# Router, shared perceptron and experts of a decoder as one straight-line stage

## The chip, the cores and the metric

One core of a Trainium2 chip runs the whole program. The metric is the device time of one execution in microseconds (us), lower is better. A core has TensorE (PE in the rows, its weight loads PEld), VectorE (DVE), ScalarE (ACT), GpSimd (POOL) and SyncE (SP, which here only issues DMAs). Each engine runs its own instructions in order; semaphores order them against each other.

## The reference, cut to what matters

The program is a two-layer decoder (16 sequences of 112 tokens, width 256). The change is in the feed-forward part of the first layer, a mixture of 8 experts with two of them per token, and one shared perceptron for all tokens:

```
flat = layernorm(x).reshape(T, D)                 # T = 1792, D = 256
probs = softmax(flat @ router_w.T)                # 8 experts
topk_p, topk_i = top_k(probs, 2)
topk_w = topk_p / maximum(topk_p.sum(-1, keepdims=True), 1e-09)
out = sum over e of _mlp(flat, w_fc[e], w_proj[e]) * combine[:, e:e + 1]
out = out + _mlp(flat, shared_fc, shared_proj)    # _mlp = square(relu(x @ up.T)) @ down.T, inner width 1024
x = x + out
```

## The kernel before, in words

The tokens stand transposed in SBUF (features on partitions): `xT` is the running sum, `hT` the normed input. Tokens go in four groups of 448 (`G`). A `Norm` object splits a group's norm into steps on several engines: `sum_halves`, `average` (a product on PE), `centre`, `square`, `sum_squares`, `variance` (PE), `invert_root`, `scale`. The first three groups are normed in the attention stage before; the last one (`tail`, group `GROUPS - 1`) is left to the router.

Three stages follow each other, each a block of its own. A block ends when all engines have reached its end (line 148 in the rows).

`router`: the last group's norm, then the logits (two products of 112 tokens by 8 experts for each of 16 sequences), then a transpose of every token row into `hrow` (PE, copied by ACT), beside a chain of 36 small operations on DVE (`link`) that picks two experts per token and numbers the slots, with five short visits to PE (lines 2044 to 2055). Its results are `routes.slot` (where each token row goes) and `routes.expert` (which expert each of 35 blocks of 128 slots uses). The block's SP also loads the raw weights of a later stage (`load_last`).

`perceptron` (named `s1`): a hardware loop (`Fori`) over three token groups. Per group, 8 up tiles (two products each, ring of four PSUM banks), ACT's relu, DVE's square, then 8 down tiles. Up tile m needs the relu of tile m - 4. Beside it POOL runs `scatter_tokens`: 32 indirect DMAs that write the token rows to the DRAM array `slots_x`, expert by expert. The fourth group's shared perceptron stands in the stage `join_and_prepare`, behind the experts.

`experts`: straight-line code over 35 blocks. SP loads rows and weights of the first three blocks (`AHEAD_BLOCKS`) when the block has begun, then one more for each result stored. PE transposes the block's rows (`turn`), 16 up products, 8 down products. DVE first measures and POOL rounds the raw weights.

In a row, a product of float32 counts as two records, so an up tile is four. The stage `join_and_prepare` later collects the results with 32 more indirect DMAs on POOL (line 1982); in it DVE's line 1272 adds what PE transposed at line 1153.

## Time and profile before

| what | value |
|---|---|
| median of 3 runs | 1936.63 us (1931.78 to 1939.18) |
| the profiled execution's own time | 1934.31 us |
| its span in the trace | 1932.5 us |
| PE busy | 1714.4 us, 89% |
| DVE / ACT / POOL busy | 887.2 / 863.5 / 325.8 us |
| mean DMA rate | 78 GB/s |

Times in the trace count from the start of the span. The three stages lie between 957 and 1350 us. A row gives the start, the duration, the engine, the line and the operation; behind it, in brackets, how long the engine sat idle before and what ended that.

### The profile page before, as it was taken

To read this page: it belongs to the slowest core of one execution; us is meant where nothing else is said; L and a number is where in the kernel's file an instruction comes from. 1 tells how busy PE (TensorE), PEld (TensorE's weight loads), DVE (VectorE), ACT (ScalarE), POOL (GpSimd) and SP (SyncE) were. 2 spreads that over 40 slices of the span, in tenths; PEclk is the share of its full clock that TensorE was granted. 3 is DMA by queue.
4 is the path that set the end of the run, shared out by engine and by line. 5 is a ranking of instruction groups with operands and counts; after the bars stand their busy time and mean duration, and the time that the engine had idled before them with its cause. 6 is when DMAs were issued, how large, how long until landed. Compare 5 with 4: busy or idle time off the path is not lost. (4 is left out here: it accounts for less than half of the span.)

```text
span 1932.5 us, 33205 instructions
## 1 busy us (share of the span) xinstructions
PE 1714.4 (89%) x13034; PEld 1118.6 (58%) x13034; DVE 887.2 (46%) x1436; ACT 863.5 (45%) x1774; POOL 325.8 (17%) x294
## 2 busy tenths in 40 slices
PE   8999999799899999999788799999487988699965
PEld 3455555554455665656553599998244666466642
DVE  4556556212545555555331211211174677276637
ACT  4243434433455555555321122222244888365656
POOL 0011212112000000000133310000601544111112
PEclk9999999999899999999878899999899899799978
DMA  6000000101100000000111499996359532000001
GB/s 235 1 1 1 1 1 1 50 0 56 29 9 17 17 10 17 18 9 2 35 48 45 170 324 329 329 322 241 94 137 223 114 75 62 20 11 11 2 1 38
DMA packets 147911, 150.03 MB, mean 78 GB/s; under 512 B 69760, under 2 KB 134976, under 8 KB 147760
## 3 DMA queue, kind: packets, MB, share of 16 engines
q1 hardware_dynamic: 144688, 140.59, 23.7%
q0 software_dynamic: 3072, 7.34, 1.3%
q8 instruction: 104, 1.70, 0.4%
q14 instruction: 47, 0.39, 0.1%
HBM read 120.39 MB, written 27.53 MB: 77 GB/s over the span
## 5 line engine op out<-in xcount | busy, mean ns | idle before, releaser
L1002 DVE TENSOR_REDUCE x_negmax<-psum 112x2 f32<-112x878 f32 x128 | 131.2, 1067 | 97.9 <-PE psum L830 97.9
L843 PEld LDWEIGHTS psum<-ident,x_probs 112*125 112x125 f32 (+1 forms) x1024 | 118.2, 169 | 76.3 <-issue 47.8
L843 PE MATMUL psum<-ident,x_probs 112*125 112x112 f32 (+1 forms) x1024 | 140.7, 276 | 15.9 <-DVE x_turned L1008 15.6
L941 ACT ACTIVATE x_probs<-psum,x_negmax 112x439 f32<-112x439 f32 x256 | 146.6, 629 | 16.8 <-DVE x_negmax L1002 16.8
L2268 DVE TENSOR_TENSOR masked<-masked 128x512 f32<-128x512 f32 x70 | 49.1, 701 | 208.9 <-ACT masked L2251 208.9
L2221 PE MATMUL psum<-experts_xb,experts_up 128*128 128x128 f32 x1120 | 132.8, 278 | 7.5 <-DMA experts_down<-in_moe_down 7.5
L2221 PEld LDWEIGHTS psum<-experts_xb,experts_up 128*128 128x128 f32 x1120 | 132.4, 194 | 9.6 <-DMA experts_down<-in_moe_down 7.9
L947 ACT COPY x_turned<-psum 125x448 f32<-125x448 f32 x128 | 68.0, 531 | 146.9 <-PE psum L843 146.0
L2229 PE MATMUL psum<-experts_down,masked 128*128 128x256 f32 x560 | 126.7, 379 | 0.0
L1462 PE MATMUL psum<-fold_full,hT 128*112 128x512 f32 x256 | 113.8, 597 | 1.3 <-DVE fold_part L1762 1.3
L2229 PEld LDWEIGHTS psum<-experts_down,masked 128*128 128x128 f32 x560 | 103.5, 190 | 12.8
L1008 DVE COPY x_turned<-psum 125x448 f32<-125x448 f32 (+1 forms) x128 | 78.8, 616 | 46.5 <-PE psum L843 44.7
L2251 ACT ACTIVATE masked<-psum 128x512 f32<-128x512 f32 x70 | 41.8, 597 | 100.8 <-PE psum L2221 100.8
L854 PE MATMUL psum<-x_turned,x_v 125*32 125x112 f32 (+1 forms) x2048 | 83.0, 267 | 1.5 <-DVE x_turned L1008 1.5
L1462 PEld LDWEIGHTS psum<-fold_full,hT 128*112 128x112 f32 x256 | 44.1, 177 | 61.4 <-issue 59.3
L1650 ACT ACTIVATE second_result<-second_result,a_rowmax 112x112 f32<-112x112 f32 x256 | 74.9, 378 | 7.5 <-DVE a_rowmax L1753 7.5
L1053 POOL TENSOR_TENSOR x_mixT<-x_mixT,x_rden 128x448 f32<-128x448 f32 x16 | 18.1, 1129 | 347.3 <-ACT x_rden L954 347.3
L1644 ACT COPY a_turned<-psum 112x448 f32<-112x448 f32 x64 | 32.4, 532 | 81.9 <-PE psum L1490 81.9
L830 PE MATMUL psum<-x_kT,x_qz 32*112 32x439 f32 x512 | 63.0, 553 | 0.0
L285 DVE TENSOR_TENSOR hT<-hT,sq 128x896 f32<-128x896 f32 x24 | 27.9, 1162 | 76.0 <-ACT sq L279 76.0
L854 PEld LDWEIGHTS psum<-x_turned,x_v 125*32 125x32 f32 (+1 forms) x2048 | 42.6, 107 | 33.7 <-issue 24.7
L1450 PE MATMUL psum<-hT,weights 128*128 128x448 f32 x128 | 55.3, 562 | 6.9 <-issue 4.0
(319 smaller groups left out, 3320.4 us busy)
## 6 DMA issues: line engine op xcount, KB each, us to landing
experts_up<-in_moe_up SPq DMA_DIRECT2D x35, 1024.0 KB, 6.0
experts_down<-in_moe_down SPq DMA_DIRECT2D x35, 1024.0 KB, 8.2
offset_rows<-join_rows SPq DMA_DIRECT2D x16, 784.0 KB, 5.3
hrow<-offset_rows SPq DMA_DIRECT2D x16, 784.0 KB, 5.3
x_ctx<-in_ctxT SPq DMA_DIRECT2D x16, 375.0 KB, 3.2
slots_x<-masked SPq DMA_DIRECT2D x1, 4480.0 KB, 21.3
experts_rows<-slots_x SPq DMA_DIRECT2D x35, 128.0 KB, 2.9
slots_y<-experts_result SPq DMA_DIRECT2D x35, 128.0 KB, 3.3
```

Source lines behind the costliest of these rows:

```text
L830: mm = nc.tensor.matmul(psum[0:T, r, 0:KEYS], qz[rows, n // BATCHES_OF % 2, e, m, t:t + T], kT[rows, n % 2, m], start=False, stop=True, sk ...
L843: mm = nc.tensor.transpose(psum[0:CHUNK_ROWS[c], 4 + i % 2, k * T:(k + 1) * T], probs[:, n % 2, slot_of_head(HG * g + k), c * CHUNK:c * CH ...
L854: mm = nc.tensor.matmul(psum[32 * k:32 * k + 32, 7, g * T:(g + 1) * T], v[0:rows, n % 2, c, HG * g + k, :], turned[0:rows, i % 4, k, :], s ...
L941: nc.scalar.activation(probs[:, n % 2, slot], psum[0:T, slot % 4, 0:KEYS], ACT.Exp, bias=negmax[:, n % 2, slot:slot + 1]).then_inc(exped.s ...
L947: nc.scalar.copy(turned[0:rows, i % 4], psum[0:rows, 4 + i % 2, 0:G].rearrange("p (k t) -> p k t", k=HG)).then_inc(copied_even.sem, 1)
L1002: nc.vector.tensor_reduce(negmax[:, n % 2, 2 * pair:2 * pair + 2], psum[0:T, b:b + 2, 0:KEYS], X, ALU.max, negate=True).then_inc(maxed.sem, 1)
L1008: nc.vector.tensor_copy(turned[0:rows, i % 4], psum[0:rows, 4 + i % 2, 0:G].rearrange("p (k t) -> p k t", k=HG)).then_inc(copied_odd.sem, 1)
L1450: mm = nc.tensor.matmul(psum[:, bank, 0:G], wt["w" + name][:, c, m * P:(m + 1) * P], src, start=c == 0, stop=c == C - 1)
L1462: mm = nc.tensor.matmul(psum[0:T, bank, :], hT[:, c, n * T:(n + 1) * T], taps, start=c == 0, stop=c == C - 1)
L1650: e = nc.scalar.activation(probs[:, n % 2, h], probs[:, n % 2, h], ACT.Exp, bias=rowmax[:, n % 2, h:h + 1])
L2221: mm = nc.tensor.matmul(psum[:, 2 * u + half, m * BLOCK:(m + 1) * BLOCK], up[:, w, c, (half * H4 + m) * P:(half * H4 + m + 1) * P], xb[:, ...
L2229: mm = nc.tensor.matmul(psum[:, 6 + u, 0:D], hidden[:, u, m, :], down[:, w, m, :], start=m == 0, stop=m == M8 - 1)
```

## The change: one block without a loop

`router`, `perceptron` and `experts` become one function `mixture` and one block. The loop over three groups is written out. PE takes the first up tile and most logits between the steps of the last norm, then the transposes and the five visits of the routing chain between the up tiles of group 0. The last norm's two sums move from POOL to DVE. For group 0 ACT makes both relu and square (`square_tile`). SP loads the experts' first weights as soon as `routes.expert` stands, and their rows when the scatter is over. The router's small tiles lie in the third weight buffer of the experts. The scatter waits until all token rows are copied. Two preloads of an activation table are gone. The rounding of the raw weights (POOL) follows the scatter, their measuring (DVE) follows the squares of group 1.

```diff
--- before.py
+++ after.py
-def perceptron(nc, stage, psum, hT, accT, w, groups, beside, load_next=None):
...
-        def group_steps(eng, step):
-            with eng.Fori(0, len(groups)) as g:
-                step(At(0, [(g, 1)]), bass.ds(g * G + groups[0] * G, G))
...
-def router(nc, psum, const, w_router, hT, routes, tail, load_last):
...
+GROUPS_BESIDE = GROUPS - 1
+RANK_AT_TILE, COUNT_AT_TILE, BLOCK_AT_TILE, OFFSET_AT_TILE, BEGIN_AT_TILE = 3, 4, 5, 6, 7
+def mixture(nc, psum, const, routes, w_router, shared, w_up, w_down, hT, accT, sq, spare, tail, zeroed, quant, raw, load_last):
...
+    hidden = sq[:].rearrange("p g c t -> p (g c t)").rearrange("p (m t) -> p m t", m=M8)
+    e_hidden = spare[:, 0:2 * M8 * BLOCK].rearrange("p (u m t) -> p u m t", u=2, m=M8)
+    e_relu = spare[:, 2 * M8 * BLOCK:3 * M8 * BLOCK].rearrange("p (u m t) -> p u m t", u=2, m=H4)
+    relu = spare[:, 2 * M8 * BLOCK:2 * M8 * BLOCK + 2 * G].rearrange("p (u t) -> p u t", u=2)
...
+        e_up = s.sb("up", [P, AHEAD_BLOCKS, C, DFF])
+        e_down = s.sb("down", [P, AHEAD_BLOCKS, M8, D])
+        e_rows = s.sb("rows", [P, AHEAD_BLOCKS, D])
...
+        room = [e_up[:, AHEAD_BLOCKS - 1].rearrange("p c n -> p (c n)"), e_down[:, AHEAD_BLOCKS - 1].rearrange("p k n -> p (k n)")]
...
+        rw = scratch(0, P, C, E)
+        plan = scratch(0, P, T + 3 * P + 1 + BLOCKS)
...
+        def shared_bank(g):
+            return 4 if g < GROUPS_BESIDE - 1 else 6
...
         @block.sync
         def _(sp):
-            def load(k):
+            loaded.inc(sp.dma_start(rw, w_router.rearrange("(c p) e -> p c e", p=P)), 16)
+            loaded.inc(sp.dma_start(plan, const["plan"]), 16)
+            sp.wait_ge(loaded.sem, 32)
+            load_last(sp)
+
+            def load_weights(k):
                 n, u = At(k), k % AHEAD_BLOCKS
...
-                sp.dma_start(rows[:, u], routes.slots_x[k * BLOCK:(k + 1) * BLOCK, :]).then_inc(rows_loaded.sem(n), 16)
-                sp.dma_start(up[:, u], w_up[bass.ds(e, 1)].rearrange("o (c p) n -> p (o c) n", p=P)).then_inc(loaded.sem(n), 16)
-                sp.dma_start(down[:, u], w_down[bass.ds(e, 1)].rearrange("o (k p) n -> p (o k) n", p=P)).then_inc(loaded.sem(n), 16)
+                sp.dma_start(e_up[:, u], w_up[bass.ds(e, 1)].rearrange("o (c p) n -> p (o c) n", p=P)).then_inc(weights_loaded.sem(n), 16)
+                sp.dma_start(e_down[:, u], w_down[bass.ds(e, 1)].rearrange("o (k p) n -> p (o k) n", p=P)).then_inc(weights_loaded.sem(n), 16)
+
+            def load_rows(k):
+                n, u = At(k), k % AHEAD_BLOCKS
+                sp.dma_start(e_rows[:, u], routes.slots_x[k * BLOCK:(k + 1) * BLOCK, :]).then_inc(rows_loaded.sem(n), 16)
...
-            sp.wait_ge(routes.scattered.sem, routes.scattered.n)
+            sp.wait_ge(chain.sem, LINKS)
             for k in range(AHEAD_BLOCKS):
-                load(k)
+                load_weights(k)
+            sp.wait_ge(routes.scattered.sem, 16 * 2 * NB)
+            for k in range(AHEAD_BLOCKS):
+                load_rows(k)
             for k in range(BLOCKS):
                 store(k)
                 if k + AHEAD_BLOCKS < BLOCKS:
-                    load(k + AHEAD_BLOCKS)
+                    load_rows(k + AHEAD_BLOCKS)
+                    load_weights(k + AHEAD_BLOCKS)
...
         @block.gpsimd
         def _(pool):
-            beside(pool)
+            Scope.clear_retired(pool)
+            pool.wait_ge(zeroed.sem, zeroed.n)
+            pool.wait_ge(rows_read, NB // 2)
+            for k in range(2):
+                pool.wait_ge(chain.sem, FIRST_SLOTS if k == 0 else LINKS - 1)
+                for b in range(NB):
+                    routes.scattered.inc(nc.gpsimd.indirect_dma_start(
+                        routes.slots_x, bass.IndirectOffsetOnAxis(ap=routes.slot[k][:, b:b + 1], axis=0), hrow[:, b, :], None), 16)
+            round_weights(nc, pool, quant, raw)
...
+            def logits(some):
+                for b in some:
+                    for c in range(C):
+                        mm = nc.tensor.matmul(psum[0:T, 6, b * E:(b + 1) * E], hT[:, c, b * T:(b + 1) * T], rw[:, c, :], start=c == 0, stop=c == C - 1)
+                return mm
+
+            def turn_pair(q):
+                if q >= 2:
+                    pe.wait_ge(rows_read, q - 1)
+                for b in (2 * q, 2 * q + 1):
+                    for c in range(C):
+                        mm = nc.tensor.transpose(psum[0:T, 4 + q % 2, (b % 2) * D + c * P:(b % 2) * D + (c + 1) * P], hT[:, c, b * T:(b + 1) * T], const["ident"][:])
+                mm.then_inc(rows_made, 1)
+
+            def up_tile(g, m):
+                if g * M8 + m >= 4:
+                    pe.wait_ge(relu_made, g * M8 + m - 3)
+                for c in range(C):
+                    mm = nc.tensor.matmul(psum[:, m % 4, 0:G], up[:, c, m * P:(m + 1) * P], hT[:, c, g * G:(g + 1) * G], start=c == 0, stop=c == C - 1)
+                mm.then_inc(up_made, 1)
+
+            def down_tile(g, k):
+                pe.wait_ge(hidden_made, g * M8 + k + 1)
+                for m in range(C):
+                    mm = nc.tensor.matmul(psum[:, shared_bank(g) + m, 0:G], down[:, k, m * P:(m + 1) * P], hidden[:, k], start=k == 0, stop=k == M8 - 1)
+                mm.then_inc(down_made, 1)
+
+            def routing(i):
+                if i == RANK_AT_TILE:
+                    flat_picks = picks.rearrange("p e b -> p (e b)")
+                    pe.wait_ge(chain.sem, PICKED)
+                    nc.tensor.matmul(psum[0:T, 7, 0:P], before, flat_picks, start=True, stop=False)
+                    nc.tensor.matmul(psum[:, 6, COUNTS:COUNTS + 1], flat_picks, ones[0:T, :], start=True, stop=True).then_inc(counted, 1)
+                if i == COUNT_AT_TILE:
+                    pe.wait_ge(chain.sem, COUNTED)
+                    nc.tensor.matmul(psum[:, 6, COUNTS + 1:COUNTS + 2], same, count, start=True, stop=True).then_inc(counted, 1)
+                if i == BLOCK_AT_TILE:
+                    pe.wait_ge(chain.sem, BLOCKED)
+                    nc.tensor.matmul(psum[:, 6, COUNTS + 2:COUNTS + 3], lower, col[:, 2:3], start=True, stop=True)
+                    nc.tensor.matmul(psum[:, 6, COUNTS + 3:COUNTS + 4], earlier, count, start=True, stop=True).then_inc(counted, 1)
+                if i == OFFSET_AT_TILE:
+                    pe.wait_ge(chain.sem, OFFSET)
+                    nc.tensor.matmul(psum[0:T, 7, 0:P], offset, const["ident"][:], start=False, stop=True).then_inc(counted, 1)
+                if i == BEGIN_AT_TILE:
+                    pe.wait_ge(chain.sem, BEGUN)
+                    nc.tensor.matmul(psum[0:1, 6, 2 * P:2 * P + BLOCKS], ones, begun, start=True, stop=True).then_inc(counted, 1)
             def turn(k):
 
                 n = At(k)
                 pe.wait_ge(*rows_loaded.after(n))
                 pe.wait_ge(*xb_ready.after(n - 1))
+                if k == 0:
+                    pe.wait_ge(shared_added, GROUPS_BESIDE - 1)
...
-            turn(0)
+            shared.wait(pe)
+            tail.average(pe, LAST, 7)
+            up_tile(0, 0)
+            pe.wait_ge(loaded.sem, 32)
+            pe.wait_ge(*tail.ready(LAST - 1))
+            logits(range(0, 5))
+            tail.variance(pe, LAST, 7)
+            logits(range(5, 12))
+            pe.wait_ge(*tail.ready(LAST))
+            logits(range(12, NB)).then_inc(scored, 1)
+            for m in range(M8):
+                if m:
+                    up_tile(0, m)
+                turn_pair(m)
+                routing(m)
+            pe.wait_ge(rows_read, NB // 2)
+            for k in range(M8):
+                down_tile(0, k)
+            for g in range(1, GROUPS_BESIDE):
+                for m in range(M8):
+                    up_tile(g, m)
+                if g == 1:
+                    pe.wait_ge(shared_added, 1)
+                else:
+                    pe.wait_ge(chain.sem, LINKS)
+                for k in range(M8):
+                    if g == GROUPS_BESIDE - 1 and k == H4:
+                        turn(0)
+                    down_tile(g, k)
+
...
-                pe.wait_ge(*loaded.after(n))
+                pe.wait_ge(*weights_loaded.after(n))
...
+                if k == 0:
+                    pe.wait_ge(shared_added, GROUPS_BESIDE)
...
-            xb_ready.start(act)
-            result_ready.start(act)
-            relu_done.start(act)
-            nc.scalar.preload_act_table(ACT.Relu)
+            for x in (xb_ready, result_ready, relu_done):
+                x.start(act)
+
+            def relu_tile(g, m):
+                i = g * M8 + m
+                act.wait_ge(up_made, i + 1)
+                if i >= 2:
+                    act.wait_ge(hidden_made, i - 1)
+                nc.scalar.activation(relu[:, m % 2], psum[:, m % 4, 0:G], ACT.Relu).then_inc(relu_made, 1)
+
+            def square_tile(m):
+
+                act.wait_ge(relu_made, m + 1)
+                act.wait_ge(*tail.ready(LAST))
+                nc.scalar.activation(hidden[:, m], relu[:, m % 2], ACT.Square).then_inc(hidden_made, 1)
+
+            tail.square(act, LAST)
+            relu_tile(0, 0)
+            tail.invert_root(act, LAST, 7)
+            act.wait_ge(chain.sem, 2)
+            nc.scalar.activation(t["prob"], t["shifted"], ACT.Exp).then_inc(exped, 1)
+            for m in range(M8):
+                if m:
+                    relu_tile(0, m)
+                square_tile(m)
+                act.wait_ge(rows_made, m + 1)
+                nc.scalar.copy(hrow[:, 2 * m:2 * m + 2].rearrange("p b d -> p (b d)"), psum[0:T, 4 + m % 2, 0:2 * D]).then_inc(rows_read, 1)
+            for g in range(1, GROUPS_BESIDE):
+                for m in range(M8):
+                    relu_tile(g, m)
...
             take(0)
+            act.wait_ge(hidden_made, GROUPS_BESIDE * M8)
...
-            dve_first(dve)
             hidden_ready.start(dve)
...
+            tail.sum_halves(dve, LAST, nc.vector)
+            nc.vector.memset(ones, 1.0)
+            tail.centre(dve, LAST, 7)
+            tail.sum_squares(dve, LAST, nc.vector)
+            tail.scale(dve, LAST)
+            dve.wait_ge(scored, 1)
+            logits = psum[0:T, 6, 0:NB * E].rearrange("p (b e) -> p b e", e=E)
...
+            def add_shared(g):
+                dve.wait_ge(down_made, M8 * (g + 1))
+                x = accT[:, :, g * G:(g + 1) * G]
+                b = shared_bank(g)
+                nc.vector.tensor_tensor(x, x, psum[:, b:b + C, 0:G], ALU.add).then_inc(shared_added, 1)
+
+            add_shared(0)
+            for g in range(1, GROUPS_BESIDE):
+                for m in range(M8):
+                    dve.wait_ge(relu_made, g * M8 + m + 1)
+                    dve.wait_ge(down_made, (g - 1) * M8 + m + 1)
+                    nc.vector.tensor_tensor(hidden[:, m], relu[:, m % 2], relu[:, m % 2], ALU.mult).then_inc(hidden_made, 1)
+                if g == 1:
+                    measure_weights(nc, dve, quant, raw)
+                add_shared(g)
             for k in range(BLOCKS):
                 n, u = At(k), k % 2
...
-                router(nc, psum, const, a["router_w"], hT, routes, n4,
-                       lambda sp: load_to_quantise(nc, sp, quant, raw, {x: a["q_" + x] for x in ("gate", "up", "down", "clip_x", "clip_down")}))
-                perceptron(nc, "s1", psum, hT, xT, shared, range(GROUPS - 1), lambda pool: scatter_tokens(nc, pool, routes, zeroed))
-                experts(nc, psum, const, routes, a["moe_up"], a["moe_down"],
-                        lambda dve: measure_weights(nc, dve, quant, raw), lambda pool: round_weights(nc, pool, quant, raw), masked[:].bitcast(F32))
+                mixture(nc, psum, const, routes, a["router_w"], shared, a["moe_up"], a["moe_down"], hT, xT, sq, masked[:].bitcast(F32), n4, zeroed, quant, raw,
+                        lambda sp: load_to_quantise(nc, sp, quant, raw, {x: a["q_" + x] for x in ("gate", "up", "down", "clip_x", "clip_down")}))
```

The order of PE's instructions, as the built programs have it, from the last norm's average to the experts. Before (names: `router_rw` is the router's weight, `s_hidden` the perceptron's inner tile, `L665` its loop):

```order
L256 MATMUL psum<-sq,averager 128x448
L273 MATMUL psum<-sq,averager 128x448
L2033 MATMUL psum<-router_rw,hT 112x8 x32
L2040 MATMUL psum<-ident,hT 112x128 x32
L2044 MATMUL psum<-router_picks,router_plan 112x128
...
L148 UNCONDITIONAL_BRANCH
...
L689 MATMUL psum<-hT,weights 128x448 x2
...
L665 COMPARE_AND_BRANCH
```

After (`mix_up` holds the router's weight and scratch, `hT,weights` is an up tile, `sq,weights` a down tile):

```order
L256 MATMUL psum<-sq,averager 128x448
L2046 MATMUL psum<-hT,weights 128x448 x2
L2031 MATMUL psum<-mix_up,hT 112x8 x10
L273 MATMUL psum<-sq,averager 128x448
L2031 MATMUL psum<-mix_up,hT 112x8 x22
L2039 MATMUL psum<-ident,hT 112x128 x4
L2046 MATMUL psum<-hT,weights 128x448 x2
...
L2052 MATMUL psum<-sq,weights 128x448 x16
L2046 MATMUL psum<-hT,weights 128x448 x16
L2052 MATMUL psum<-sq,weights 128x448 x8
L2083 MATMUL psum<-ident,mix_rows 128x128 x2
```

The first up tile and ten of the 32 logit products now stand ahead of the variance, the transposes are spread over the up tiles, and the experts' first turn stands in the middle of the last down tiles. No branch is left between them.

The order of SP's instructions behind the raw weights, after the change (`mix_down` is the experts' second weight, `mix_rows` the rows of a block):

```order
L2322 DMA raw_weights<-in_q_down 128x2x704
L1982 TENSOR_LOAD block_expert
L1984 ISA
L1984 DMA mix_up<-in_moe_up 128x2x1024
L1985 DMA mix_down<-in_moe_down 128x8x256
...
L1989 DMA mix_rows<-slots_x 128x256 x3
L1995 DMA slots_y<-mix_result 128x256
```

Before, the rows of each block were loaded directly ahead of its weights, behind the block's branch.

## Rows read from the trace of the kernel before

**Rows 1.** Timeline, PE, the three stages: start, duration, engine, line, idle before.

```profile
995.96 14.29 PE L689 MATMUL psum<-hT,weights 128*128 x32 [3.38 <-ACTq L74]
1010.09 12.19 PE L695 MATMUL psum<-s_hidden,weights 128*128 128x448 f32 x32
1022.11 6.18 PE L689 MATMUL psum<-hT,weights 128*128 x16
1029.45 1.77 PE L689 MATMUL psum<-hT,weights 128*128 x4 [1.16 <-issue]
1038.60 7.88 PE L689 MATMUL psum<-hT,weights 128*128 x12 [7.38 <-issue]
...
1058.34 12.19 PE L689 MATMUL psum<-hT,weights 128*128 x32
...
1094.83 5.82 PE L2221 MATMUL psum<-experts_xb,experts_up 128*128 128x128 f32 x32 [7.47 <-DMA experts_down<-in_moe_down]
...
1104.15 3.73 PE L2221 MATMUL psum<-experts_xb,experts_up 128*128 128x128 f32 x32
...
1343.24 3.73 PE L2221 MATMUL psum<-experts_xb,experts_up 128*128 128x128 f32 x32
```

**Rows 2.** Windows: stretch, length, busy time by engine, PEclk, DMA share, GB/s.

```profile
970.00:982.00 12.00, 11.84 (x64) 11.84 (x65) 0.11 (x1) 0.00 (x0) 0.00 (x0) 0.50 0.01 1
...
1000.00:1022.00 22.00, 22.00 (x60) 11.15 (x59) 5.00 (x8) 3.80 (x7) 17.12 (x17) 1.00 0.29 88
...
1101.00:1340.00 239.00, 239.00 (x1651) 225.28 (x1650) 46.29 (x66) 60.31 (x133) 18.81 (x25) 1.00 0.95 322
```

**Rows 3.** Timeline, the last norm, 957 to 970.

```profile
957.35 0.06 DVE L2077 MEMSET router_ones<- 128x1 f32 x1 [0.35 <-PEq L148]
...
960.64 1.83 PE L256 MATMUL psum<-sq,averager 128*128 128x448 f32 x2 [4.49 <-POOL sq L252]
...
965.84 1.86 PE L273 MATMUL psum<-sq,averager 128*128 128x448 f32 x2 [3.37 <-POOL sq L269]
...
969.01 1.09 DVE L285 TENSOR_TENSOR hT<-hT,sq 128x896 f32<-128x896 f32 x1 [5.42 <-ACT sq L279]
```

**Rows 4.** Timeline, logits, transposes and the routing chain.

```profile
970.16 12.11 PE L2033 MATMUL psum<-router_rw,hT 128*112 128x8 f32 x64 [2.46 <-DVE hT L285]
...
982.13 5.74 PE L2040 MATMUL psum<-ident,hT 128*112 128x128 f32 x32
...
987.88 0.38 DVE L2101 TENSOR_TENSOR router_picks<-router_pick 112x128 f32<-112x128 f32 x1
...
994.59 0.18 DVE L2131 TENSOR_SCALAR block_expert<-psum 1x35 uint32<-1x35 f32 x1
```

**Rows 5.** Timeline, POOL's scatter and ACT's relu in the second group.

```profile
996.05 1.15 POOL L1974 DMA_INDIRECT slots_x<-hrow,slot  x1 [30.26 <-SPq L148]
...
1008.19 1.20 POOL L1974 DMA_INDIRECT slots_x<-hrow,slot  x1 [0.30 <-issue]
...
1028.85 0.54 ACT L709 ACTIVATE s_relu<-psum 128x448 f32<-128x448 f32 x1 [18.02 <-PE psum L689]
...
1036.36 0.94 POOL L1974 DMA_INDIRECT slots_x<-hrow,slot  x1 [0.30 <-issue]
...
1038.01 0.54 ACT L709 ACTIVATE s_relu<-psum 128x448 f32<-128x448 f32 x1 [8.61 <-remote]
```

**Rows 6.** Timeline, the stage behind the experts, beside the last indirect DMAs.

```profile
1380.50 0.41 PE L1153 MATMUL psum<-ident,hrow 112*128 112x112 f32 x2 [3.38 <-issue]
...
1398.82 0.39 DVE L1272 TENSOR_TENSOR xT<-xT,psum 128x224 f32<-128x224 f32 x1 [18.38 <-remote]
1399.24 0.62 DVE L252 TENSOR_TENSOR sq<-xT 128x448 f32<-128x448 f32 x1
```

**Rows 7.** DMA queues in the window 1011 to 1084: packets, MB, share.

```profile
DMA packets 1056, 2.52 MB, mean 35 GB/s; under 512 B 352, under 2 KB 352, under 8 KB 1056
## 3 DMA queue, kind: packets, MB, share of 16 engines
q0 software_dynamic: 1056, 2.52, 11.2%
```

More of the change, by code:

```diff
@@ L2137 @@
[L2137 to L2155 removed]
+        ones = scratch(0, P, 1)
```

300 lines of the change are left out of this document (91 added, 209 removed).

## The prediction

> **What bounds the kernel now.** I read the windows first, then the timeline of each engine through the three stages. In the 35 expert blocks PE is busy 239 of 239 us at the full clock [rows 2], and a block takes (1343.24 - 1104.15) / 33 = 7.24 us [rows 1]. Nothing there changes, so the change can win only ahead of them, between the barrier at 957.3 [rows 3] and the first expert product at 1094.83 [rows 1]. PE waits or crawls there in four places. The last norm goes back and forth between engines for 13 us, with PE idle in it [rows 3]. The logits and transposes run for 12.1 and 5.7 us at half clock while nothing else does; the routing chain goes on to 994.59 [rows 2, 4]. The perceptron's second group takes 1058.34 - 1022.11 = 36.2 us, where two rounds of 12.02 us (1022.11 - 1010.09) are its work: 12.2 us are lost [rows 1]. And from about 1082.4 (1058.34 and two rounds) to 1094.83 PE has only one turn to do and waits for the experts' weights; then the first block runs at half clock, 9.32 us to the next block in place of 7.24 [rows 1].
>
> **The loss in the second group** decides most of the answer. PE has finished the first up tile of that group near 1023.8 (22.11 and four records of 0.376). ACT's relu of it starts at 1028.85, and the next at 1038.01, though its tile was done some 12 us before [rows 1, 5]. PE can take only four tiles ahead, so it stops. All of this lies beside the 32 indirect DMAs, 996.05 to 1036.36 [rows 5]. The same sight stands in the stage behind the experts, which has no loop there: PE transposes at 1380.50, and DVE, which waits for that transpose alone, starts at 1398.82, 18.4 us idle [rows 6]. I read both as one thing: while POOL issues indirect DMAs, what waits for PE's results can be released many microseconds late. PE is then held only where it needs an answer, so in the up tiles, not in the down tiles.
>
> Another reading is the loop: its second pass needs code from further back. The third pass, which branches back in the same way, loses nothing (1058.34 is on time) [rows 1]. The DMA queues moved no instruction packet from 1011 to 1084 [rows 7]. So I give the branch little. The Trainium skill, page "Runtime: NRT & Kernel Launch", section "Instruction fetch mechanics", says the opposite: a taken branch whose target is not in the current two-page window makes the engine wait for a DMA fetch, and kernels should be unrolled. By it the whole 12.2 us would go with the loop; the absence of instruction packets in this trace speaks against it here.
>
> **The change part by part.**
>
> 1. The norm. The sum moves to DVE, 0.62 us [rows 6], and can start at the barrier, 957.35 [rows 3]. PE's average then starts at about 958.1 in place of 960.64. PE's own list to the end of the logits is now the limit: average 1.8 [rows 3], one up tile at half clock 3.0 (twice 1.5), 64 logit records 12.1 [rows 4], variance about 1.6. Together 18.5, so they end at 976.6 and not at 982.3. The norm itself fits: variance done near 968.5, scale about 2.4 later (965.84 + 1.86 to 970.10) [rows 3], at 970.9, while the middle logits run to 973.6. The clock stayed at 0.50 all through the logits [rows 2]; should the up tile lift it, 4 us more are won. Gain 5.7.
>
> 2. Group 0's up tiles under the routing. From 976.6 PE has 7 up tiles (10.5), the transposes (5.7), seven small products (0.36 each, like two records of the transposes [rows 4], 2.5) and a cold start (14.29 - 12.19 = 2.1 [rows 1]). That is 20.8; the transposes behind the clock's rise are shorter, so I take 20, to 996.6. The picks stand 988.26 - 982.3 = 6 us after the logits [rows 4], and PE asks for them only after three up tiles: no wait. But each of the chain's later visits to PE now waits behind an up tile and a pair, 2.2 us. So the experts' numbers stand at about 997.5, not earlier than before (994.8), and the scatter starts at about 997, where it was at 996.05 [rows 4, 5]. What is won is that 12 us of up tiles are done by then. ACT has relu, square and copy, under 1.8 us, in each 2.2.
>
> 3. Down tiles of group 0 to 1009, group 1 to 1033.1, group 2 to 1057.2, the turn in it 0.4: PE is free for the experts at 1057.6 if nothing stalls. The first weights (6 DMAs of 1 MB, issued from about 998) have until then, and the rows have from the scatter's end, about 1041, to the turn at 1051. DVE's measuring of the raw weights lies beside group 1's down tiles (12 us), POOL's rounding behind the scatter; neither is asked for by PE. The two table loads (ACT) lay beside waits already: zero.
>
> 4. The barriers and the cold first block. The block follows at once and at full clock: 9.32 - 7.24 = 2.1 us.
>
> Without a stall: 1094.83 - 1057.6 + 2.1 = 39.3 us. The stall stays, because the scatter stays and lies at the same time: 997 to 1038. Before it cost 12.2. It can now fall on group 1's up tiles (1009 to 1021) and the first ones of group 2 (1033). From below: if the late releases begin 26 us into the scatter as before (1022), only group 2 meets them, for 3 to 6 us. From above: in the later stage they held three times in a row until the DMAs ended; if group 1 is caught at its fourth tile (1015) and freed at about 1042.5, what is left is 18.1 + 24.1 + 0.4 and a cold start of 2.1, so the experts begin at 1087. I take 12, the size of the one stall in the same code. Sum: 39.3 - 12 = 27 us. Against the profiled execution's 1934.3 that is 1907; against the median, which lies 2.3 higher, 1909.5.
>
> **The rivals.**
>
> - The stall goes or is small, by the loop's branch or by timing. For it: the unrolled code, and half of before's scatter passed without a late release (to 1022). Against it: the loopless stage [rows 6]. Gain 33 to 39, with a warmer start 43: 1894 to 1904. Chance 0.25.
> - The long stall: group 1 is held until the scatter is over. For it: the 18.4 us of [rows 6], and the weights' 6 MB now move beside the scatter. Then 1094.83 - 1087.1 + 2.1 = 10 us gain, with half of it held 20: 1917 to 1927. Chance 0.23.
> - Slower: the scatter itself is stretched. A DMA issue took 1.20 + 0.30 us beside a busy DVE where it took 0.94 + 0.30 otherwise [rows 5]. With all 32 at 1.5 us it lasts 48 in place of 41 us, and on top of the long stall the experts start at 1094: no change. PE waits in order, so everything behind the turn waits for the rows too. It is slower from the point where the scatter ends later than about 1052 (1.7 us a DMA); if the 6 MB beside it double the issue, to 2.5 us, it ends at 1077, and the time is about 1960. Nothing in the trace shows such a rate. Chance 0.05, and 0.07 for no change.
> - The forecast, a stall between 6 and 17 us: 1902 to 1916. Chance 0.40.
>
> **How the numbers follow.** The likeliest case gives 1909. The range takes the forecast, the small stall and the long one but for their ends: 1894 to 1926. About 0.5%, 9.7 us, is what a measurement of this kernel can tell from no change. Faster by more than that: 0.40 + 0.25 + nearly all of 0.23 = 0.87. Within it: 0.07 and the end of the long stall, 0.08. Slower: 0.05.
>
> **What would show it.** PE's logits end near 976.6 and the seven small products stand between up tiles, with no wait over 1 us. POOL's first indirect DMA starts at 995 to 999, 32 of them at 1.25 us. The weights' issues stand beside it. ACT's relus of group 1 or 2 start several microseconds after their tile, and PE's up tiles show the gap; the down tiles show none. The first expert product starts at 1066 to 1074, at full clock, and the blocks keep 7.24 us. I am wrong if the gap is missing (then the start is at 1058), if the up tiles of group 1 end only when the scatter does (1087), if the scatter's issues are longer than 1.25 us, or if the routing chain falls behind the up tiles so far that the third group waits for it.

## The result, and the profile after

The changed kernel took 1904.23 us (median of 4, 1901.80 to 1906.97) where the kernel before took 1934.72 us beside it (median of 4): a ratio of 0.984, 95% interval 0.982 to 0.986, 30.5 us less. The profiled execution took 1906.97 us with a span of 1905.1 us. The forecast was 1909.0 us, with 1894 to 1926 as its range.

The runs of this work were made on four occasions, not all on one chip, and the kernel before itself took 1934.7, 1891.9, 1933.6 and 1932.7 us on them. Only kernels of one occasion are compared below, except where a sentence says otherwise; they are called the first (the result above) to the fourth occasion.

PE through the changed stage, its timeline, which answers to [rows 1, 3, 4]:

```profile
957.85 0.99 PE L256 MATMUL psum<-sq,averager 128*128 128x448 f32 x2 [2.03 <-DVE sq L252]
958.67 3.06 PE L2046 MATMUL psum<-hT,weights 128*128 128x448 f32 x4
961.53 2.37 PE L2031 MATMUL psum<-mix_up,hT 128*112 128x8 f32 x20
...
964.59 7.30 PE L2031 MATMUL psum<-mix_up,hT 128*112 128x8 f32 x44
971.75 1.08 PE L2039 MATMUL psum<-ident,hT 128*112 128x128 f32 x4
972.62 3.19 PE L2046 MATMUL psum<-hT,weights 128*128 128x448 f32 x4
...
990.61 12.29 PE L2052 MATMUL psum<-sq,weights 128*128 128x448 f32 x32 [1.12 <-ACT hrow L2165]
1002.74 12.43 PE L2046 MATMUL psum<-hT,weights 128*128 128x448 f32 x32
1015.00 6.18 PE L2052 MATMUL psum<-sq,weights 128*128 128x448 f32 x16
...
1037.89 4.66 PE L2052 MATMUL psum<-sq,weights 128*128 128x448 f32 x8 [3.76 <-DVE sq L2273]
1042.39 12.19 PE L2046 MATMUL psum<-hT,weights 128*128 128x448 f32 x32
...
1066.66 3.73 PE L2124 MATMUL psum<-mix_xb,mix_up 128*128 128x128 f32 x32
...
1074.13 3.73 PE L2124 MATMUL psum<-mix_xb,mix_up 128*128 128x128 f32 x32
...
1313.21 3.73 PE L2124 MATMUL psum<-mix_xb,mix_up 128*128 128x128 f32 x32
```

The logits now end at 971.75, group 0's down tiles begin at 990.61, and its whole perceptron is done at 1002.74. Group 1 (up tiles from 1002.74, down tiles from 1015.00) runs to 1042.39, 39.65 us where two rounds are 24.05: the gap of [rows 1] is still there, 15.6 us of it. Then nothing holds PE until the experts, and their first block is nearly a normal one, 7.47 us; the blocks keep (1313.21 - 1074.13) / 33 = 7.24 us.

Windows (us; the columns are busy time and instructions of PE, PEld, DVE, ACT and POOL, then PE's granted clock, DMA share and GB/s), against [rows 2]:

```profile
961.50:963.90 2.40, 2.40 (x22) 2.37 (x21) 0.11 (x1) 0.54 (x1) 0.00 (x0) 0.85 0.94 310
...
968.00:971.70 3.70, 3.70 (x21) 3.70 (x22) 0.00 (x0) 0.00 (x0) 0.00 (x0) 0.50 0.24 93
```

Behind the one up tile the clock is granted at 0.85 under the first logits; under the last ones it is back at 0.50.

ACT and POOL in the timeline, against [rows 5], and DVE in the stage behind the experts, against [rows 6]:

```profile
1012.80 0.54 ACT L2147 ACTIVATE masked<-psum 128x448 f32<-128x448 f32 x1 [3.02 <-PE psum L2046]
1020.52 0.54 ACT L2147 ACTIVATE masked<-psum 128x448 f32<-128x448 f32 x1 [7.18 <-issue]
1029.62 0.54 ACT L2147 ACTIVATE masked<-psum 128x448 f32<-128x448 f32 x1 [8.56 <-remote]
1036.63 0.98 ACT L2147 ACTIVATE masked<-psum 128x448 f32<-128x448 f32 x2 [6.47 <-remote]
...
991.44 1.15 POOL L2019 DMA_INDIRECT slots_x<-hrow,slot  x1 [41.79 <-ACT hrow L2165]
...
1030.74 0.95 POOL L2019 DMA_INDIRECT slots_x<-hrow,slot  x1 [0.30 <-issue]
...
1362.43 0.39 DVE L1192 TENSOR_TENSOR xT<-xT,psum 128x224 f32<-128x224 f32 x1 [14.23 <-remote]
```

PE has all eight up tiles of group 1 done at 1015.0. ACT's relus of the last four start at 1020.52, 1029.62 and (two) 1036.63. PE, by now in the down tiles, waits for what comes of them. The scatter runs from 991.44 to 1031.69, 32 DMAs at 1.25 us.

### The profile page after: what moved, and what is told of

Same layout as the page of the kernel before. It is cut to its first block and busy times, and to the rows that moved or that the text cites. A ratio compares the mean times of both kernels' runs of the same rounds, so it can differ in the third digit from the quotient of the medians.

```text
span 1905.1 us, 33059 instructions
## 1 busy us (share of the span) xinstructions
PE 1710.4 (90%) x13034; PEld 1113.8 (58%) x13034; DVE 883.6 (46%) x1430; ACT 865.5 (45%) x1780; POOL 324.0 (17%) x292
## 3 DMA queue, kind: packets, MB, share of 16 engines
q1 hardware_dynamic: 144688, 140.59, 24.1%
## 5 line engine op out<-in xcount | busy, mean ns | idle before, releaser
L763 PE MATMUL psum<-ident,x_probs 112*125 112x112 f32 (+1 forms) x1024 | 140.8, 276 | 15.9 <-DVE x_turned L928 15.6
L2124 PEld LDWEIGHTS psum<-mix_xb,mix_up 128*128 128x128 f32 x1120 | 130.6, 192 | 2.1 <-issue 0.4
L2124 PE MATMUL psum<-mix_xb,mix_up 128*128 128x128 f32 x1120 | 130.7, 275 | 0.0
L2134 PE MATMUL psum<-mix_down,masked 128*128 128x256 f32 x560 | 126.9, 379 | 0.0
L2134 PEld LDWEIGHTS psum<-mix_down,masked 128*128 128x128 f32 x560 | 103.6, 190 | 13.0 <-DVE masked L2282 0.4
```

Source lines behind the costliest of these rows:

```text
L763: mm = nc.tensor.transpose(psum[0:CHUNK_ROWS[c], 4 + i % 2, k * T:(k + 1) * T], probs[:, n % 2, slot_of_head(HG * g + k), c * CHUNK:c * CH ...
L2124: mm = nc.tensor.matmul(psum[:, 2 * u + half, m * BLOCK:(m + 1) * BLOCK], e_up[:, w, c, (half * H4 + m) * P:(half * H4 + m + 1) * P], xb[: ...
L2134: mm = nc.tensor.matmul(psum[:, 6 + u, 0:D], e_hidden[:, u, m, :], e_down[:, w, m, :], start=m == 0, stop=m == M8 - 1)
```

## The experiments

### The scatter and the late releases, first try

Theory A: what holds PE in group 1 is that its results are released late beside POOL's indirect DMAs. Four kernels were run on the second occasion. The changed kernel without the scatter, so that the experts work on rows of zeros (SP then waits only for that zeroing before it loads rows):

```diff
-            sp.wait_ge(routes.scattered.sem, 16 * 2 * NB)
+            sp.wait_ge(zeroed.sem, zeroed.n)
...
-            for k in range(2):
-                pool.wait_ge(chain.sem, FIRST_SLOTS if k == 0 else LINKS - 1)
-                for b in range(NB):
-                    routes.scattered.inc(nc.gpsimd.indirect_dma_start(...), 16)
+            pool.wait_ge(chain.sem, LINKS - 1)
             round_weights(nc, pool, quant, raw)
```

> The changed kernel without the 32 indirect DMAs that scatter the token rows; the experts compute on the zeroed rows instead, with the same blocks and weights. Theory A (results of PE are released late while POOL issues indirect DMAs): group 1 takes 24.1 us in place of 39.65, the first expert product starts near 1051, and the time falls by about 15.5 us, to 1888.5. Rival B (the hold is from the order of the code, such as the square on DVE behind the sum of group 0, or the experts' weight loads beside): group 1 stays at 35 to 40 us and the time moves by under 4 us.

The 32 DMAs as plain ones to fixed places, on POOL's queue:

```diff
-                    routes.scattered.inc(nc.gpsimd.indirect_dma_start(...), 16)
+                    routes.scattered.inc(nc.gpsimd.dma_start(routes.slots_x[(k * NB + b) * T:(k * NB + b + 1) * T, :], hrow[:, b, :]), 16)
```

> The changed kernel with each indirect DMA replaced by a plain one of the same size (112 rows of 1 KB to a fixed place), issued by POOL at the same point. Theory A1 (it is the software-made descriptors of POOL's queue): group 1 still takes 35 to 42 us. Theory A2 (it is the indirect form alone): group 1 takes 24 to 26 us, and the first expert product starts near 1051.

The same 32 plain DMAs on SP's queue, behind the first weights (POOL's loop over them is gone, as in the first kernel):

```diff
+            sp.wait_ge(rows_read, NB // 2)
...
+                    routes.scattered.inc(sp.dma_start(routes.slots_x[(k * NB + b) * T:(k * NB + b + 1) * T, :], hrow[:, b, :]), 16)
```

> The changed kernel with the 32 scatters replaced by plain DMAs of the same size on SP's queue, behind the first weights. Theory A1: no late release, group 1 at 24 to 26 us, first expert product 1051 to 1056. Rival C (any DMA traffic of this size beside the up tiles holds PE's releases): group 1 still takes over 30 us.

And the kernel before without its scatter:

```diff
-            sp.wait_ge(routes.scattered.sem, routes.scattered.n)
...
-                perceptron(nc, "s1", psum, hT, xT, shared, range(GROUPS - 1), lambda pool: scatter_tokens(nc, pool, routes, zeroed))
+                perceptron(nc, "s1", psum, hT, xT, shared, range(GROUPS - 1), lambda pool: pool.wait_ge(zeroed.sem, zeroed.n))
```

> The kernel before with its loop over three groups, without the 32 indirect DMAs (the experts compute on zeroed rows). Theory A: the second pass of the loop starts its relu on time, the second group takes 24.1 us in place of 36.2, and the time falls by 12 us, to about 1923. Rival D (the branch back of the loop costs it): the second group still takes about 36 us, and the time does not move.

Measured: 1859.87 us (4 runs, ratio to the kernel before 0.984, 0.980 to 0.988), 1858.93 and 1858.36 us (one run each), and 1890.29 us (10 runs, ratio 1.000, 0.998 to 1.001). Group 1 took 24.05 us in the first three, the second group 24.05 us in the last. Taken alone, this seems to say that the scatter costs nothing. But look at the stage behind the experts, whose 32 indirect gathers all four kernels keep. The trace of the changed kernel without the scatter, DVE and then PE in that stage:

```profile
1334.09 0.39 DVE L1192 TENSOR_TENSOR xT<-xT,psum 128x224 f32<-128x224 f32 x1 [0.50 <-PE psum L1073]
...
1309.53 9.26 PE L1059 MATMUL psum<-hT,weights 128*128 128x448 f32 x24 [2.78 <-PEq L148]
...
1338.88 1.37 PE L1087 MATMUL psum<-hT,weights 128*128 128x448 f32 x3 [0.85 <-DVE hT L285]
```

From its first up tile to the first product of line 1087 that stage takes 29.35 us here, and 58.99 us (1323.19 to 1382.18) in the changed kernel on the first occasion; DVE's waits for its first transposes are 0.5 to 2.1 us, where the longest was 14 to 18. Here nothing is released late even beside indirect DMAs, so the kernel before has no gap to lose either (hence 1.000), and the four runs can't tell theory A from its rivals. What they do show: late releases are no property of the program alone. In the kernel before itself the stage behind the experts takes 57.97 us on the first occasion (1353.22 to 1411.19) and 31.15 us here without the scatter (1341.04 to 1372.19). These 26.8 us and the 12.2 us of the second group are 39.0 of the 42.8 us by which the kernel before is faster here.

### The scatter and the late releases, second try

The first and the fourth kernel were run again on the fourth occasion.

> The changed kernel without its 32 scattering DMAs, so the experts work on rows that are zero; all else stands. The same file as the first experiment, sent again so that it meets a chip where the kernel before takes near 1935 us. Theory A: group 1 takes 24.1 us in place of 36 to 40, the first expert product starts near 1051 to 1053, and the time is 12 to 15 us less than the changed kernel's. Rival (the weights' 6 MB or the measuring of the raw weights beside group 1 is what holds it): group 1 stays at over 30 us and the time within 4 us.

> The kernel before, with its loop, without its 32 scattering DMAs, so the experts work on rows that are zero. The same file as the fourth experiment, sent again for the same reason. Theory A: its second group takes 24.1 us in place of 36.2, branch and all, and the time is about 12 us less than the kernel's before, a ratio of 0.994. Rival (the loop's branch back costs the 12 us): the second group still takes 34 to 37 us, ratio 1.000.

The first took 1884.85 us (4 runs, ratio 0.977, 0.973 to 0.981), the second 1919.09 us (5 runs, ratio 0.993, 0.990 to 0.995), 13.6 us less than the kernel before. PE's timeline of the changed kernel without the scatter:

```profile
956.45 0.99 PE L256 MATMUL psum<-sq,averager 128*128 128x448 f32 x2 [2.03 <-DVE sq L252]
...
1001.33 12.19 PE L2042 MATMUL psum<-hT,weights 128*128 128x448 f32 x32
...
1025.39 12.19 PE L2042 MATMUL psum<-hT,weights 128*128 128x448 f32 x32
...
1049.66 3.73 PE L2120 MATMUL psum<-mix_xb,mix_up 128*128 128x128 f32 x32
...
1305.96 10.71 PE L1059 MATMUL psum<-hT,weights 128*128 128x448 f32 x24 [2.78 <-PEq L148]
...
1364.36 1.74 PE L1087 MATMUL psum<-hT,weights 128*128 128x448 f32 x4 [0.85 <-DVE hT L285]
```

and of the kernel before without it:

```profile
1021.21 12.19 PE L689 MATMUL psum<-hT,weights 128*128 x32
...
1045.26 12.19 PE L689 MATMUL psum<-hT,weights 128*128 x32
...
1080.39 5.57 PE L2220 MATMUL psum<-experts_xb,experts_up 128*128 128x128 f32 x32 [6.44 <-DMA experts_down<-in_moe_down]
```

Both groups fall to 24.05 us. The stage behind the experts, which keeps its 32 gathers, takes 58.40 us (1305.96 to 1364.36) and not 29.35: results are released late on this occasion too, and the loss is gone only where the indirect DMAs are. The loop's branch back is still in the second kernel, so it costs nothing that shows, and that rival is out. The weights' 6 MB and the measuring of the raw weights are still in the first one, so by themselves they hold nothing. From the norm's average to the first expert product the changed kernel takes 93.2 us here; with the scatter it takes 108.8 (957.85 to 1066.66, first occasion) or 105.7 (third, below): the scatter costs it 12.5 to 15.6 us, and it cost the kernel before 13.6. Without any scatter the change is worth 1919.09 - 1884.85 = 34.2 us. The saving doesn't depend on the stall. Whether plain DMAs of POOL would release late as well on such a chip wasn't tried.

### The changed kernel with parts undone

On the third occasion, beside the changed kernel itself.

> The changed kernel itself, unchanged, beside the kernel before on the same chip. Where the kernel before takes near 1892 us, and its second group has no gap, theory A (the saving in front of the experts comes from the order of work, and is nearly the same with and without late releases) expects group 1 in 24.1 us, the first expert product near 1052 us, and a time of 1860 us, a ratio of 0.983. The rival, that the scatter costs something in the changed kernel even there, expects 1865 to 1875 us and a gap in group 1 or 2. Where the kernel before takes near 1935 us, both expect group 1 in 36 to 42 us and 1904 us.

1896.46 us (4 runs, 1891.94 to 1902.01), ratio 0.980 (0.978 to 0.983): results are released late here, and the same program takes 1896 us where it took 1904 on the first occasion. Its timeline is the base for the next three:

```profile
956.36 0.99 PE L256 MATMUL psum<-sq,averager 128*128 128x448 f32 x2 [2.04 <-DVE sq L252]
...
989.12 12.29 PE L2052 MATMUL psum<-sq,weights 128*128 128x448 f32 x32 [1.12 <-ACT hrow L2165]
1001.25 12.19 PE L2046 MATMUL psum<-hT,weights 128*128 128x448 f32 x32
...
1037.76 12.19 PE L2046 MATMUL psum<-hT,weights 128*128 128x448 f32 x32
...
1062.03 3.73 PE L2124 MATMUL psum<-mix_xb,mix_up 128*128 128x128 f32 x32
```

**The router's work first, then group 0.** (ACT's order follows.)

```diff
             tail.average(pe, LAST, 7)
-            up_tile(0, 0)
+            tail.variance(pe, LAST, 7)
             pe.wait_ge(loaded.sem, 32)
...
-            logits(range(12, NB)).then_inc(scored, 1)
+            logits(range(NB)).then_inc(scored, 1)
             for m in range(M8):
-                if m:
-                    up_tile(0, m)
                 turn_pair(m)
+            for m in range(M8):
                 routing(m)
+            for m in range(M8):
+                up_tile(0, m)
```

> Undoes one part: in the stage without a loop the logits, all 16 transposes and the routing chain's seven small products come ahead of every up tile of group 0, as they did before; the shared groups are still unrolled, the barriers are still gone and the weights are still loaded beside. Theory: the interleaving is worth what the order says, the up tiles under the chain: the down tiles of group 0 start 12 to 15 us later than in the changed kernel, and so do the first expert product and the end: +12 to +15 us on the changed kernel, most of its saving gone on a chip where nothing is released late. Where releases are late the scatter starts up to 6 us earlier, against work that starts later, and the difference may fall to 8 us. Rival: the saving is that of the missing barriers, the loop and the early weights, and the interleaving gives under 4 us.

1914.81 us (4 runs), ratio 0.991 (0.989 to 0.993), 18.4 us more than the changed kernel.

```profile
956.35 0.99 PE L256 MATMUL psum<-sq,averager 128*128 128x448 f32 x2 [2.03 <-DVE sq L252]
...
1000.92 12.19 PE L2052 MATMUL psum<-sq,weights 128*128 128x448 f32 x32
1012.95 5.80 PE L2046 MATMUL psum<-hT,weights 128*128 128x448 f32 x15
...
1034.59 8.52 PE L2046 MATMUL psum<-hT,weights 128*128 128x448 f32 x16 [14.27 <-ACT masked L2144]
...
1054.96 12.19 PE L2046 MATMUL psum<-hT,weights 128*128 128x448 f32 x32
...
1079.24 3.73 PE L2121 MATMUL psum<-mix_xb,mix_up 128*128 128x128 f32 x32
```

The down tiles of group 0 start 11.8 us later, as the order says. The scatter now catches group 1 in its up tiles: PE stands still behind its fourth tile until 1034.59, and the group takes 42.0 us where it took 36.5. So 17.2 us are lost by the first expert product: 11.8 of order, 5.4 of a worse meeting with the scatter. The expectation that the stall would give some of it back was wrong in sign. The interleaving is about half of the whole saving, 18.4 of 37.2 us on this occasion. The other half (DVE's sums, the barriers and the wait for weights behind them) is read from the timelines; no run takes it apart.

**The first weights behind the scatter.**

```diff
-            for k in range(AHEAD_BLOCKS):
-                load_weights(k)
             sp.wait_ge(routes.scattered.sem, 16 * 2 * NB)
             for k in range(AHEAD_BLOCKS):
                 load_rows(k)
+                load_weights(k)
```

> Undoes one part: the weights of the first three expert blocks are issued behind the scatter, with the blocks' rows, and not beside the picks. Theory: the scatter's last DMA is issued near 1031 us, the six transfers of 1 MB land in 15 to 20 us from there, the first block's two within 8, and the first product is due at 1052 (no late releases) or 1067 (late releases): 0 to +2 us on the changed kernel. Rival: the weights are what the experts would wait for, as in the kernel before, whose PE waited from about 1082 to 1095; then +5 to +12 us.

1903.88 us (4 runs), ratio 0.983 (0.980 to 0.986). The median is 7.4 us above the changed kernel's, more than the 0 to 2 us expected, but the intervals of the two ratios overlap (0.980 to 0.986 and 0.978 to 0.983), and the timeline places no loss in front of the experts:

```profile
957.83 1.00 PE L256 MATMUL psum<-sq,averager 128*128 128x448 f32 x2 [2.03 <-DVE sq L252]
...
1063.62 3.73 PE L2123 MATMUL psum<-mix_xb,mix_up 128*128 128x128 f32 x32
```

That is 105.79 us from the average to the experts, and 105.67 in the changed kernel; to the first up tile of the stage behind the experts it is 362.45 us (957.83 to 1320.28) and 362.34 (956.36 to 1318.70). What the profiled executions differ by lies outside the changed stage. Loading the first weights early is worth nothing here: from the scatter's end (1032.06) to the first expert product PE has 31.6 us of other work and of stall, which hide them anyway. Whether they would be hidden without the stall isn't shown.

**No up tile ahead of the logits.**

```diff
-            up_tile(0, 0)
             pe.wait_ge(loaded.sem, 32)
...
-                if m:
-                    up_tile(0, m)
+                up_tile(0, m)
```

> Group 0's first up tile no longer stands ahead of the logits, but behind them with the others. Theory (that dense tile is what raised the clock under the logits): the 64 logit records go back to 0.189 us each, 12.1 us in all, the granted clock is 0.50 under them as in the kernel before, and the down tiles of group 0 start 1 to 4 us later than in the changed kernel. Rival: the clock rises for another reason, the logits take 9.7 us as in the changed kernel, and the down tiles start at the same time or up to 1 us earlier or later.

1906.39 us (one run). The timeline:

```profile
958.82 0.99 PE L256 MATMUL psum<-sq,averager 128*128 128x448 f32 x2 [2.03 <-DVE sq L252]
961.21 3.90 PE L2031 MATMUL psum<-mix_up,hT 128*112 128x8 f32 x20 [1.40 <-DMA mix_up<-in_plan]
964.97 1.84 PE L273 MATMUL psum<-sq,averager 128*128 128x448 f32 x2
966.60 8.25 PE L2031 MATMUL psum<-mix_up,hT 128*112 128x8 f32 x44
...
995.82 12.29 PE L2052 MATMUL psum<-sq,weights 128*128 128x448 f32 x32 [1.13 <-ACT hrow L2161]
```

The logits take 3.90 + 8.25 = 12.15 us again, all at a granted clock of 0.50, and the down tiles start 37.0 us behind the average in place of 32.8: 4.2 us later. The logits are 2.5 us of it (12.15 against 2.37 + 7.31), the variance 0.8, and PE idles 1.40 us ahead of the logits for a table that the tile used to cover; 0.5 us of these 4.7 comes back behind the logits. One dense tile ahead of the logits is what lifted the clock for them.

### Fewer signals from PE

In the changed kernel's late stretch ACT's relus start further and further behind their tiles. Theory B: PE's increments stand in a queue that drains slowly, so fewer of them would wait less.

```diff
-                mm.then_inc(up_made, 1)
+                if g == 0:
+                    mm.then_inc(up_made, 1)
+                elif m % 2:
+                    mm.then_inc(up_made, 2)
...
-                mm.then_inc(down_made, 1)
+                if k == M8 - 1:
+                    mm.then_inc(down_made, M8)
```

> The changed kernel with fewer signals from PE in the stage without a loop, and no other edit: groups 1 and 2 tell of two up tiles at once (one increment by 2), and a group's eight down tiles are told of once, at the last (an increment by 8). Theory B (beside the indirect DMAs PE's increments are released one behind another, some 3.5 us apart at first and 7 to 9 later, so what counts is how many stand in that queue): group 1 then has 4 such increments for its up tiles in place of 8, the relus start within 1 to 4 us of their tiles, group 1 takes 25 to 30 us in place of 36 to 40, and the time is 6 to 12 us less than the changed kernel's, on a chip where the kernel before takes near 1935 us. Where it takes near 1892 us: no difference. Rival (each release is late by a time of its own until the DMAs end, however many there are): group 1 takes 36 to 40 us as before, within 2 us of the changed kernel.

The second kernel has the same edit also in the stage behind the experts.

> The kernel with fewer signals, and the same edit also in the stage behind the experts (its up tiles told of in pairs, its eight down tiles at the last). Theory B: that stage has the same queue beside its 32 gathers, and loses about 28 us there; 16 of its some 25 increments become 5, so it gives 8 to 15 us more than the kernel with the edit in one stage. Rival: the transposes between the tiles need an answer each, are late by a time of their own, and it gives under 3 us. Near 1892 us for the kernel before: no difference.

On the fourth occasion 1900.75 us (4 runs, ratio 0.985, 0.981 to 0.988) and 1900.88 us (4 runs, ratio 0.985, 0.981 to 0.988). ACT and PE of the first of the two:

```profile
1001.88 0.98 ACT L2151 ACTIVATE masked<-psum 128x448 f32<-128x448 f32 x2 [15.39 <-issue]
1007.05 0.98 ACT L2151 ACTIVATE masked<-psum 128x448 f32<-128x448 f32 x2 [4.20 <-remote]
1016.88 0.98 ACT L2151 ACTIVATE masked<-psum 128x448 f32<-128x448 f32 x2 [8.85 <-remote]
1030.88 0.98 ACT L2151 ACTIVATE masked<-psum 128x448 f32<-128x448 f32 x2 [13.03 <-remote]
...
998.67 12.26 PE L2046 MATMUL psum<-hT,weights 128*128 128x448 f32 x32
...
1037.58 12.19 PE L2046 MATMUL psum<-hT,weights 128*128 128x448 f32 x32
```

The pairs of tiles are done at 1001.8, 1004.8, 1007.8 and 1010.8; the relus follow after 0.1, 2.3, 9.1 and 20.1 us. In the changed kernel (third occasion) the relus of the same tiles, the second, fourth, sixth and eighth, follow after 0.2, 3.0, 10.6 and 21.6 us. So the lag goes with the tile and not with the number of signals sent before it, and group 1 takes 38.9 us, inside the 36.5 to 39.7 of the changed kernel. Theory B falls. The stage behind the experts gains 0.7 us by the same edit (57.9 to 57.2 us from its first up tile to the first product of line 1087, 1089 in the second), not 8 to 15. Neither kernel is shown to be faster than the changed one.

What fits all the traces is simpler: the last late result is released a few us after POOL's last indirect DMA, 4.9 us behind it in the changed kernel (1031.69 to 1036.63), 2.7 here (its last DMA ends at 1028.15), 5.3 with the router first (1028.67 to 1033.99). In the kernel before, the last DMA ends at 1037.30 [rows 5], and the last late relus, of tiles done by 1028.1, start 4.2 us later:

```profile
1041.47 0.98 ACT L709 ACTIVATE s_relu<-psum 128x448 f32<-128x448 f32 x2 [2.92 <-remote]
```

Behind the experts, in all ten traces of the three occasions, DVE's last late start comes 3.7 to 5.7 us after the last gather. So PE is free a few us behind the last DMA, plus what it still has to do then. This is read from the traces and was not tested by itself; why results are held back stays open.

## Why the prediction was right

The time was forecast within 5 us. That is closer than its parts were: the first two terms gave 5.9 us more than forecast and the stall took 3.6 us more, so part of the closeness is luck. Times by which the changed kernel is ahead on the first occasion, from [rows 1, 4] and the timeline above: end of the logits 10.4 (982.13 against 971.75), down tiles of group 0 19.5, up tiles of group 1 19.4, up tiles of group 2 16.0, first expert product 28.2, last expert block 30.0.

1. **The norm and the logits**: forecast 5.7 us, measured 10.5. This is the mis-sized term. The sum did start when the barrier fell (average 957.85, forecast 958.1), and PE's list was the limit. But the logits took 9.7 us and not 12.1, the variance 1.0 and not 1.6, because the up tile lifted the clock. The average took 0.99 us and not 1.8; that isn't the tile's doing, since it took 0.99 without the tile too. PE had idled 2.03 us before it, and 4.49 in the kernel before [rows 3], whose 1.8 us I had carried over. The prediction named 4 us for the clock and did not take them, since the clock had stayed at 0.50 under the logits of before; without the tile 4.2 us are lost, 3.3 of them by the clock under logits and variance.
2. **The up tiles under the routing**: forecast 20 us, measured 18.9 (971.75 to 990.61). The seven small products stand between the tiles with no wait; the one wait is 1.12 us for ACT's last copy, ahead of the down tiles. The scatter came at 991.44, 4.6 us before it did in the kernel before, outside the 995 to 999 that I had named: since the whole list was shorter, the token rows were copied and the slots known earlier.
3. **The three groups**: down tiles, up tiles and the turn are as costed, and nothing that PE asks for waits for the weights, DVE's measuring or POOL's rounding. Where the first weights stand turned out to be free either way.
4. **The barriers and the cold first block**: forecast 2.1 us, measured 1.85 (9.32 against 7.47). The wait for weights ahead of it is gone: 1082.4 to 1094.83 before, nothing now. Without the scatter the kernel before still waits there (6.44 us for the weights, and then 5.57 us for the first block's up products, which take 3.73 in a later block), so that part belongs to the change and not to the stall.
5. **The stall**: forecast 12 us, measured 15.6 on the first occasion and 12.5 on the third (1001.25 to 1037.76). The cause was right, by the second try. The place was not: I wrote that PE is held in the up tiles, not in the down tiles, and that the down tiles show no gap. They show all of it. PE's up tiles of group 1 ran through (12.43 us), since only ACT's first four relus are needed for them: the fourth was 4 us late, at 1012.80, and just early enough for the eighth tile. The down tiles need what comes of the last four. I had overlooked that a down tile waits for an answer too, through relu and square. The gap stands in the up tiles where the scatter is further on when group 1 begins: 24.1 us with the router first (988.86 to 1012.95), for 5.4 us more, and 11.3 us in the changed kernel (989.95 to 1001.25, same occasion).

The sum closes: 27.3 forecast, plus 4.8 and 1.1 for terms 1 and 2, minus 3.6 for the stall, is 29.6; measured are 30.0 at the last expert block, 27.4 in the span of the two profiled executions and 30.5 between the medians.

Of the rivals, the small stall did not come. Its first reason fails, since the loop's branch costs nothing. Its second is half true: here too the first part of the scatter passes almost in time, and the first relu that is 4 us late starts at 1012.80, 21 us into it, but group 1 lay right there. The Trainium skill's rule on taken branches (page "Runtime: NRT & Kernel Launch", section "Instruction fetch mechanics"), weighed in the prediction, has no price here: the pass behind the branch takes 24.05 us, two rounds of work. That doesn't contradict the rule, which speaks of targets outside a window; no run shows whether this loop's start lies inside. The long stall had its mechanism right, held until the DMAs end, but when the last result came PE had only one or two down tiles of group 1 left, and group 2, and not a group and a half. The stretched scatter did not come: 1.25 us a DMA beside the weights' 6 MB.

## What to carry to other kernels

Put work that PE can do in any order between the steps of a chain that other engines set; it was worth 11.8 us here, 17.2 with what the stall added, and dense tiles also keep the clock up for the small products between them. An early load gives nothing where the work behind it is long enough to hide it (31.6 us here). A stall that ends with another queue's last transfer is sized by that end and by the work that is left then, so ask what an earlier start of the waiting work will meet there.

## What the runs showed of the hardware

- **Late releases came on three of the four occasions.** There, beside 32 indirect DMAs of POOL, results of PE are released up to some 20 us late, the last ones 2.7 to 5.7 us after the last DMA. On the second occasion, on another chip than the third and the fourth, the trace shows nothing of the kind (29.35 against 58.99 us for the stage behind the experts, with the same 32 gathers), and the kernel before is 42.8 us, 2.2%, faster than on the first. Whether it is the chip that makes the difference isn't shown. Halving the number of PE's signals left the lags, and the 38.9 us of the group, as they were.
- **The clock fell under small products.** With the up tile ahead, the first 20 logit records took 2.37 us and the next 44 took 7.30 us, in windows of granted clock 0.85 and at last 0.50 (the lower level, 1.2 GHz), while PE was busy without a gap; the dense tiles behind brought it back, 3.19 us for the first and 1.67 for the second. The Trainium skill, page "TensorE: Matmul & The Clock Gate", section "Part 1: The HAM clock gate", says that the clock is throttled by default and that PE's activity releases it. The dense tiles agree. The small products don't: the logits of the kernel before kept PE busy 11.84 of 12.00 us at 0.50 [rows 2], and those here ran without a gap while the clock fell.
- **The same program differed by 0.4% between two occasions that both release late**: 1904.23 and 1896.46 us for the changed kernel, with 1934.72 and 1933.61 us for the kernel before beside them.
